# A transformer block on one core: the folded keys, roots, last keys and the last convolution window at other places

## The reference

```python
def _L1_attn_ref(x, w_qkv, w_proj, b_proj, w_dwc, b_dwc):      # focused linear attention, 16 heads of 16
    ...
    q = _norm_last(jax.nn.relu(q) + EPS); k = _norm_last(jax.nn.relu(k) + EPS)
    q = _norm_last(q ** FOCUS);           k = _norm_last(k ** FOCUS)          # FOCUS = 3
    kv = jnp.einsum('bhnd,bhne->bhde', k, v)
    z = 1.0 / (jnp.einsum('bhnd,bhd->bhn', q, k.sum(axis=2)) + EPS)
    out = jnp.einsum('bhnd,bhde,bhn->bhne', q, kv, z)
    ...
    conv = xp[:, 0:N] * w_dwc[:, 0] + xp[:, 1:N + 1] * w_dwc[:, 1] + xp[:, 2:N + 2] * w_dwc[:, 2] + b_dwc
    return jnp.einsum('bnc,oc->bno', out + conv, w_proj) + b_proj

def _L1_xattn_ref(image_features, text_features, Wq, bq, Wk, bk, Wv, bv):     # cross attention, one head
    query = image_features @ Wq + bq;  key = text_features @ Wk + bk;  value = text_features @ Wv + bv
    weights = jax.nn.softmax(query @ key.T / 16, axis=-1)
    return weights @ value
```

## Time and profile before

| what | value |
|---|---|
| median of three runs | 1662.14 us (1662.04 to 1662.39) |
| the profiled execution | 1662.17 us, its span 1660.3 us |
| mean granted TensorE clock | 0.996 of full speed |
| PE busy | 1585.8 us (96%) |
| DVE busy | 1481.6 us (89%) |
| ACT busy | 1313.1 us (79%) |
| POOL busy | 417.4 us (25%) |

### The profile page before, as it was taken

The page is one execution under the profiler, slowest core; times in us unless marked ns, Lnnn a source line. Parts: engine busy times, 40 slices in busy tenths (PEclk is TensorE's granted clock), DMA queues, the critical chain, the costliest instruction groups (busy, mean ns, idle before and its releaser), DMA issues. The chain is left out here.

```text
span 1660.3 us, 36679 instructions
## 1 busy us (share of the span) xinstructions
PE 1585.8 (96%) x14540; PEld 641.6 (39%) x14540; DVE 1481.6 (89%) x2152; ACT 1313.1 (79%) x2558; POOL 417.4 (25%) x671
## 2 busy tenths in 40 slices
PE   6999999999999999999999999999998999889997
PEld 3542222322233222323322222222224576757773
DVE  6899999999999999998999999999975887688876
ACT  4618999879988989898899999999995565635644
POOL 5801110111321412310311111111003455533302
PEclk9999999999999999999999999999999999999999
DMA  4001001001100210110221100101002000024551
GB/s 149 14 7 20 14 15 14 14 14 20 34 14 14 38 29 14 20 27 14 64 79 14 27 14 19 23 14 27 8 8 90 1 2 1 1 42 93 95 104 51
DMA packets 148026, 52.33 MB, mean 32 GB/s; under 512 B 137424, under 2 KB 146128, under 8 KB 147600
## 3 DMA queue, kind: packets, MB, share of 16 engines
q1 hardware_dynamic: 147152, 48.62, 14.3%
q10 hardware_dynamic: 704, 1.38, 0.2%
HBM read 14.07 MB, written 2.10 MB: 10 GB/s over the span
## 5 line engine op out<-in xcount | busy, mean ns | idle before, releaser
L968 DVE TENSOR_REDUCE mxp<-ps_m 128x2 f32<-128x1024 f32 (+2 forms) x928 | 1049.0, 1195 | 41.4 <-PE ps_m L747 40.0
L897 ACT ACTIVATE work<-ps_s 128x512 f32<-128x512 f32 x1856 | 1001.7, 598 | 76.6 <-PE ps_s L771 48.9
L797 PE MATMUL ps_av<-work,vst 128*32 128x256 f32 x7424 | 592.8, 391 | 14.7 <-ACT avs L904 12.3
L771 PE MATMUL ps_s<-qb,k_stack 50*128 50x512 f16 x1856 | 565.6, 382 | 0.5 <-ACT v_rows L915 0.3
L747 PE MATMUL ps_m<-k_stack,qa 48*128 48x512 f16 (+1 forms) x2048 | 534.3, 358 | 2.3 <-PEq L1123 0.5
L797 PEld LDWEIGHTS ps_av<-work,vst 128*32 128x32 f32 x7424 | 147.0, 108 | 383.2 <-ACT work L897 321.6
L771 PEld LDWEIGHTS ps_s<-qb,k_stack 50*128 50x128 f16 x1856 | 119.6, 94 | 378.6 <-ACT work L897 321.3
L747 PEld LDWEIGHTS ps_m<-k_stack,qa 48*128 48x128 f16 x2048 | 108.2, 93 | 21.5 <-DVE mxp L968 14.8
L616 POOL TENSOR_SCALAR mtmp<-negm 128x16 f32<-128x16 f32 x32 | 8.2, 255 | 390.4 <-DVE negm L973 390.3
L602 POOL COPY vst<-v_rows 128x1024 f32<-128x1024 f32 (+1 forms) x32 | 30.6, 956 | 144.4 <-PE ps_av L797 144.3
L682 POOL TENSOR_TENSOR q_rows<-avs,rc 128x256 f32<-128x256 f32 x31 | 19.2, 620 | 173.2 <-DVE rc L979 173.2
(11 more groups left out here) (441 smaller groups left out, 1985.5 us busy)
## 6 DMA issues: line engine op xcount, KB each, us to landing
x_res<-in_x SPq DMA_DIRECT2D x4, 512.0 KB, 8.1
w_experts<-in_w_experts SPq DMA_DIRECT2D x1, 2048.0 KB, 8.1
out<-x_res SPq DMA_DIRECT2D x8, 256.0 KB, 2.1
v_rows<-in_ctx_c SPq DMA_DIRECT2D x1, 1664.0 KB, 7.2
work<-in_ctx_t SPq DMA_DIRECT2D x1, 1456.0 KB, 15.6
ctx_n<-in_ctx_n SPq DMA_DIRECT2D x1, 1248.0 KB, 7.8
w_qkv<-in_w_qkv ACTq DMA_DIRECT2D x1, 768.0 KB, 8.5
w_qkv<-in_w_qkv SPq DMA_DIRECT2D x1, 768.0 KB, 4.2
```

The lines of the kernel that those rows point to most:

```text
L771: pe.matmul(ps_s[:, bank, :], STACKS[part(n)][rows, group(n) * PAIRS + j, t * P:t * P + P], qb[n % 2][rows, :, j, :], start=True, stop=Tru ...
L797: m = pe.matmul(ps_av[32 * h:32 * h + 32, cols], vst[n % 2][:, t, h, :], pbuf[(tau[n] + t) % 2][:, h, cols], start=(t == 0 and half == 0), ...
L897: a.activation(pbuf[g % 2][:, h, :], ps_s[:, b, :], ACT.Exp, scale=factor).then_inc(s["exp"], 1)
L968: v.tensor_reduce(dst, src, AX.X, ALU.max).then_inc(s["mred"], 1)
```

## The change

Six things are done.

- The fold is computed in the expert stage. PE does `folded_keys` in steps 2 and 3, `folded_bias` and `folded_side` in step 4; ACT copies the results out of PSUM at the end of step 5 (`hold_fold`); POOL makes the replicated bias `wide` in step 2.
- DVE takes the three peaks at the end of steps 9, 10 and 11. PE transposes them in step 16 (`turned_peaks`) and spreads them over the partitions in step 17 (`spread_peaks`); DVE's work for these is at the end of steps 17 and 18 (`peaks_over_rows`, `scales`), and ACT scales the fold behind the last step (`scale_fold`).
- ACT loads the table of Sqrt in step 15 with an instruction on one column (`warm`), before `focused_rows(10)`. The roots of the last two groups stand behind `focused_rows(11)` in step 16 and behind `squared(11)` in step 17.
- `outer(13)` on PE moves from step 20 to step 21, before `values(15)`.
- POOL adds the output bias of tiles 13 to 15 at the start of the linear attention stage, not in the last steps of the expert stage.
- In the linear attention stage the last window has 512 columns, its left taps are done by ACT and POOL, and DVE's and PE's streams are arranged anew around it.
- Three products that nobody reads stand at the end of PE's stream in that stage (`idle_products`).

```diff
@@ projection_experts_queries, tensor @@
+            def spread_peaks():
+                pe.wait_ge(s["fold"], 5)
+                pe.matmul(ps_w, ones[0:3, :], diag[:, :], start=True, stop=True).then_inc(s["made"], 1)
...
+                if n == 4:
+                    folded_bias()
                 if n < T:
                     experts(n, 2)
...
                 if n + 1 < T:
                     logits(n + 1)
+                if n in (2, 3):
+                    folded_keys(n - 2)
+                if n == 4:
+                    folded_side()
                 if n < T:
                     experts(n, 3)
+                if f == T - 1:
+                    outer(f - 2)
                 if f is not None:
                     values(f, c)
                 if f == T - 1:
                     last_queries(f, c)
-                if n - LAG - 1 >= 0:
+                if n == T:
+                    turned_peaks()
+                if n == T + 1:
+                    spread_peaks()
+                if n - LAG - 1 >= 0 and f != T - 2:
                     outer(n - LAG - 1)
@@ projection_experts_queries, scalar @@
+            def hold_fold():
+                e.wait_ge(s["made"], 4)
+                e.copy(fold[:, :, :], ps_f).then_inc(s["held"], 1)
+                e.activation(side[:, 0:D + 1], ps_side, ACT.Copy, scale=1.0 / 16.0).then_inc(s["held"], 1)
+                e.copy(raw[:, :], ps_b).then_inc(s["held"], 1)
+
+            def scale_fold():
+                e.wait_ge(s["fold"], SCALED)
+                e.activation(fold[:, :, :], fold[:, :, :], ACT.Copy, scale=part[:, 0:1]).then_inc(s["scaled"], 1)
...
                 if n < T:
                     weigh(n, 1)
+                if n == T - 1:
+                    e.activation(warm[:, :], gain[:, :], ACT.Sqrt)
...
                     focused_rows(f + 1)
+                if n == T:
+                    root(FOCUSED_NORMS, 3, s["fvar"], s["froot"])
...
                 if f is not None:
                     squared(f)
+                if n == T + 1:
+                    root(FOCUSED_NORMS, 4, s["fvar"], s["froot"])
...
                     value(f)
-                if n >= T - 1 and norm_at(FOCUSED_NORMS, n) is not None:
-                    root(FOCUSED_NORMS, norm_at(FOCUSED_NORMS, n), s["fvar"], s["froot"])
+                if n == 5:
+                    hold_fold()
...
+            scale_fold()
             squared_last()
@@ projection_experts_queries, gpsimd @@
-                if f is not None and f < T - 1:
+                if f is not None and f < HELD:
                     plus(f)
@@ projection_experts_queries, vector @@
+                    if 9 <= n <= 11:
+                        peak_of(n - 9)
                 else:
                     relu(f)
...
                         focused_norm_back(len(FOCUSED_NORMS) - 1)
+                        peaks_over_rows()
+                    if n == T + 2:
+                        scales()
@@ linear_attention @@
-    WINDOWS = [(0, 2), (2, 4), (4, 6), (6, 7), (7, 8)]
-    LATE = 3
-    CONV = [(1, 1), (2, 2), (3, 3), (5, 3), (7, 3)]
+    WINDOWS = [(0, 2), (2, 4), (4, 6), (6, 8)]
+    SPLIT = 3
+    CONV = [(1, 1), (2, 2), (3, 3), (5, 3)]
+    HELD = 13
@@ linear_attention, tensor @@
-            folded_keys()
             pe.wait_ge(s["set"], 5)
             numerators(0)
             numerators(1)
-            folded_bias()
-            turn(0)
...
-            turned_peaks()
-            turn(2)
-            numerators(4)
-            spread_peaks()
...
+            for p in range(6):
+                turn(p)
+                numerators(p + 2)
+            project(0)
             turn(6)
-            project(0)
+            project(1)
             turn(7)
-            project(1)
             project(2)
             project(3)
             turn_first()
             project(4)
+            project(5)
             query_first()
-            project(5)
             project(6)
             project(7)
+            idle_products(pe, ps_n[:, 1, 0, 0:D], ident[:, :], w[:, 0, :], 3)
@@ linear_attention, scalar @@
-            middle(3, 0)
-            middle(3, 1)
             out(7)
-            middle(4, 0)
-            middle(4, 1)
+            window_taps(3)
             a.wait_ge(s["var"], 1)
@@ linear_attention, gpsimd @@
+            for n in range(HELD, T):
+                g.tensor_tensor(x[:, n, :], x[:, n, :], bias[:, :], ALU.add).then_inc(s["bias"], 1)
-            for i in range(LATE):
+            for i in range(len(WINDOWS)):
                 left(i, 0)
                 left(i, 1)
-                right(i)
+                if i < SPLIT:
+                    right(i)
@@ linear_attention, vector @@
-            left(3, 0)
-            left(3, 1)
             v.wait_ge(s["pad"], 1)
+            add(3)
+            add(4)
             right(3, 0)
             right(3, 1)
-            add(3)
-            left(4, 0)
-            left(4, 1)
-            right(4, 0)
-            right(4, 1)
-            add(4)
             add(5)
+            add(6)
             first_low()
-            add(6)
             add(7)
```

196 lines of the change are left out of this document (83 added, 113 removed).

## The result

The changed kernel takes 1669.01 us (median of six runs, 1666.52 to 1669.68) against 1662.09 (six, 1660.54 to 1663.98): 1.0039 times the time before, 95% interval 1.0026 to 1.0052. It is slower by about 7 us (4.3 to 8.6 by the interval), where 1664.8 was forecast and 1668.0 was the top of the range. The profiled execution took 1669.36 us, 7.2 us more than that of before.

The account below looks back on a forecast made before the run. PE was taken to bound the expert stage, a chain over engines the linear stage. 2.84 + 0.1 + 3.5 - 4.9 - 0.4 = +1.14 us, +2.6 with the clock's fall: 1664.8 us, range 1659.0 to 1668.0.

Parts of the forecast that it names:

- Fold: Expert stage, steps 2 to 4: folded keys, bias and side on PE add 2.84 us, bounds 2.0 and 4.6.
- Table load: Step 15: load of 1.28 us plus 0.15 for the warm instruction stalls PE by 1.43, bounds 1.0 and 1.6.
- a drain: Rival, step 15: the table load drains as in the page's rule, 1.4 us more, 1666.2; chance 0.04.
- Roots: Steps 16 and 17: PE's waits for pxf of 0.27 and 1.25 go, -1.52 us.
- The wait for `pdiag`: Step 17: PE's spreading product waits for DVE's chain after the relu, a stall of 3.0 to 3.1 us.
- the clock behind it: After step 17's stall PE falls to 1.2 GHz for 3.0 us; half, 1.5 us, is lost.
- Scales: Step 18: a dozen DVE instructions, 1.5 to 2.8 us, of which 0.7 delays PE, bounds 0 and 1.4.
- Saving 3.1 + 1.8 = 4.9 at the last statistics: Linear attention stage: root 3.1 us earlier and 1.8 less DVE work behind it, bounds 3.5 and 7.5.
- The first `middle` [...] comes 0.85 + 2.20 earlier, less 0.4: Linear stage's head: folded keys, bias and side gone, less DVE's first shares, put the first middle 2.66 us earlier.
- a rival with 0.17: The linear stage's head falls to 1.2 GHz too, costing 1.5 us more, 1666.3; chance 0.17.
- the tail's 1.8: Linear stage behind the root: four tap pairs (3.5 us) leave DVE, two 512-column instructions (1.7) come in.
- 0.4 for a gain in the next stage: Unread products at the linear stage's end shorten PE's idle before the next stage: -0.4 us, bounds 0 and -1.5.

Follow-up runs that it names:

- e12: Changed kernel with each product of folded_keys in steps 2 and 3 done twice: 1670.96 us, 1.0056.
- e6: Changed kernel without the warm instruction, the two roots behind value(9) and value(10) as in the kernel before: 1670.08 us, 1.0051.
- e4: Changed kernel with six products that nobody reads before the wait of the spreading product in step 17: 1667.66 us, 1.0036.
- e2: Changed kernel with five products that nobody reads between project(3) and turn_first: 1667.65 us, 1.0040.
- e13: Changed kernel, order kept, with unread products before the pdiag wait, on both sides of the barrier and before turn_first: 1664.44 us, 1.0020.
- e11: Changed kernel with spread_peaks and scales one step later, turn_first behind project(5), query_first behind project(6), unread products around the barrier: 1661.16 us, 0.9998.
- e8: Changed kernel with POOL's output bias of tiles 13 to 15 added in the expert stage's last steps, as before: 1670.25 us, 1.0043.
- e5: Changed kernel with turn_first behind project(5) and query_first behind project(6) on PE: 1666.21 us, 1.0026.
- e7: Changed kernel with the last four tiles' convolution in two 256-column windows, DVE's left taps and that part's old orders: 1669.21 us, 1.0047.
- e16: Kernel before with only the three unread products at the end of PE's linear attention stream added: 1662.51 us, 1.0001.

## Why the prediction was wrong

The mechanisms up to the linear stage were right, and their sizes too. Fold: 2.74 for 2.94 at step 15, and e12 shows that PE's work passes through. Table load 1.47 for 1.43; nothing of a drain shows, for 1.28 and the warm instruction account for it. Roots as forecast (-0.27 and -1.25), though e6 finds the pair of load and moved roots worth about nothing by then. The wait for `pdiag` 3.42 for 3.0 to 3.1; the clock behind it 1.68 for 1.5 (e4: 1.67). Scales were put at 0.7 and cost nothing visible, since queries of step 20 are shifted by 7.60 as are those of step 19. The -0.33 up to the start of the stage is near the -0.4 of POOL's bias adds, but the stretch from queries of step 20 to that start takes 9.55 us here and 9.92 in e2 and e4 with the same instructions, so it shows little. That the clock's 1.5 came so near is partly luck: it was half of one row's 3.0, and other executions paid up to 3.1.

The step that failed is "Saving 3.1 + 1.8 = 4.9 at the last statistics". They came 0.60 us later, counted from the start of the stage. The forecast had named a linear stage shorter by less than 3 us as a sign that it was wrong. Times in us behind the start of the stage:

| landmark | before | after | e13, full clock | forecast change |
|---|---|---|---|---|
| first `middle` | 8.54 | 8.60 | 6.64 | -2.66 |
| root of the first tiles | 25.03 | 24.69 | 22.75 | -3.1 |
| last statistics | 37.40 | 38.00 | 34.42 | -4.9 |

So 5.5 us are missing at the last statistics, and the clock is 3.6 of them. It failed in four ways.

First, the head. "The first `middle` [...] comes 0.85 + 2.20 earlier, less 0.4". At full clock it comes 8.54 - 6.62 = 1.9 earlier (e11; 6.64 in e13), so the term was too great by 0.8. PE's numerators start 0.3 us earlier and not 0.85, since they wait for `lbd`, and e8 shows that POOL's bias adds beside it cost 0.6, which is the difference. At half clock, as in the changed kernel, it comes no earlier at all. That this stretch could fall to 1.2 GHz stood as a rival with 0.17, and it should have been the likeliest case: my own row showed that 2.2 to 2.4 us of idle time were followed by a fall, and 2.4 was worked out for the place. It became 3.0. Even so e6 kept its clock behind the same 3.01 us: the fall was likely, not certain.

Second, the tail's 1.8. I counted DVE's instructions and not who stands behind whom. `turn_first` waits for `oxn`, and projects 4 and 5, which could start 2.1 us earlier (e5), stand behind `turn_first`. The root wasn't even last: it ended at 1462.71, and DVE came to the reciprocal for `oxn` only at 1463.24, behind a tap, an add and statistics and with no idle time. e5 undoes the order and gets 2.8 us, but mostly through the clock; what the order alone cost is 0.3 in the traces, because DVE is then what PE waits for. From the first `middle` to the last statistics the kernel at full clock (e13) takes 1.1 us less than before, where 2.2 was forecast. e7 shows that with this order the window of 512 is worth nothing.

Third, that wait of 3.7 us lowers the clock once more. No term and no rival had it; e2 prices it at 1.6 us in the trace, though its times alone don't show that.

Fourth, DVE's norm of the first tiles ran beside POOL's taps. Two small operations and `oxn` took 2.6 us more than alone; e7, where POOL is done earlier, has two of the three at 0.17 and 0.41 us. DVE couldn't have passed the root in any case, so by an estimate from these rows `oxn` was late by 1.1 us at most for it: 0.5 from the root's end to the reciprocal, and 0.6 of its own length. How much of that reached the end no run separates.

The sum of the two traces: 5.5 missing at the last statistics, less 0.7 for costs before the stage that were put too high, 0.4 for a gain in the next stage that didn't come there, and -0.6 behind it, are the 4.6 us by which the profiled execution passed the forecast of a change of 2.6. By medians the miss is 4.2. The clock's three falls are 5.3 us in the traces, of which I had counted 1.5. The -0.4 for the next stage isn't seen either: its first product stands 1.39 us behind the start of the last statistics in both traces, and e16, which makes the clock there full, shows no gain.

Not settled: why the clock falls at one idle time of 1.5 us (e1, e16) and not at another, and why it held behind 3.01 us in e6. The same instructions behind the same idle time do both, so idle time makes a fall likely and doesn't decide it: of the ten traces with 3.0 us at the head nine fell, and the numerators took 3.20 to 4.00 us in these.

## What to carry over

When work is taken out of a stage, ask what PE does at its head in place of it: an idle time that grows past 2 us may cost the clock, and with it as much as was saved. A wait in an in-order stream costs what stands ready behind it; here moving one small transpose behind two ready projects gave 2.8 us, most of it by keeping the clock, and one product of three columns by one step 3.9. One profiled execution can gain or lose 1 to 2 us by where the clock falls, so compare stretches between landmarks before putting a difference down to an edit. And where DVE is given less, look at what POOL does beside the rest.
